# Giving every step of a decoder layer its own moment in the order of each engine's queue, and loading the ffn weights earlier

## The reference

```python
x = x + attn(layernorm(x))           # 16 heads of 8; k and v from a latent of 32; rope; causal softmax
x = x + xattn(layernorm(x), ctx)     # 8 heads of 64 over 32 context rows
x = x + ffn(layernorm(x))            # fp4 quantise-dequantise of x, weights and hidden; silu(gate) * up; 352 wide
# fp4: scale = max(max|block of 16| / 6, 1e-12); q = nearest of the fp4 grid to x / scale, times scale
```

## Time and profile before

| | us |
|---|---|
| timed runs, median (lowest to highest) | 427.41 (425.4 to 429.64) |
| profiled execution, first to last instruction | 431.1 |
| first maxima of slot 0 on TensorE | 34.59 |
| first scores of slot 0 on TensorE | 47.19 |
| last store's data ready | 429 |

### The profile page before, as it was taken

How to read it: one execution, slowest core, us unless ns; L and a number is a source line. 1 busy time by engine, 2 the same in 40 slices (tenths; PEclk the granted TensorE clock), 3 DMA queues, 4 the chain that set the end, 5 groups by cost and what they waited for, 6 DMA issues and landing times.

```text
span 431.1 us, 6518 instructions
## 1 busy us (share of the span) xinstructions
PE 295.3 (69%) x1790; PEld 144.0 (33%) x1790; DVE 301.2 (70%) x1137; ACT 177.1 (41%) x327; POOL 194.2 (45%) x374
## 2 busy tenths in 40 slices
PE   1702655777888788787868687787878846657454
PEld 1300233332343222324333334344343314436233
DVE  5426749472666546878886898989978356787872
ACT  5320345563544454443555454454446313222111
POOL 4200216761133534545384745535447353745653
PEclk9999999996766655886997798989969869766696
DMA  6079000043030025002100260030000000000000
GB/s 186 0 207 209 1 0 2 2 149 74 1 75 1 0 76 147 2 2 59 23 8 0 81 149 6 3 79 3 9 6 2 8 0 8 6 1 7 2 13 18
DMA packets 20835, 17.50 MB, mean 41 GB/s; under 512 B 1920, under 2 KB 20224, under 8 KB 20800
## 3 DMA queue, kind: packets, MB, share of 16 engines
q1 hardware_dynamic: 20272, 16.50, 15.7%
q10 hardware_dynamic: 528, 0.59, 0.5%
HBM read 9.62 MB, written 7.34 MB: 39 GB/s over the span
## 4 chain that ended last, share of the span: by engine, by line
PE 36%; DVE 30%; issue 10%; POOL 9%; DMA 7%; ACT 5%; SPq 1%; POOLq 0%; DVEq 0%; ACTq 0%
DVE summed L832 7%; PE pvp L1116 7%; PE st L1105 4%; PE mxp L1081 4%; DMA ks<-parts_dram 3%; PE mxp L1016 3%; DVE space L766 2%; PE misc L1180 2%; DMA parts_dram<-parts 2%; POOL space L473 2%; DVE space L763 2%; PE misc L1195 2%; PE pvp L1127 2%; DVE space L746 2%; ACT probs L633 2%
## 5 line engine op out<-in xcount | busy, mean ns | idle before, releaser
L832 DVE CUSTOM_DVE_ANT_0 summed<-mxp,causal 128x512 bf16<-128x512 f32 (+3 forms) x256 | 114.0, 485 | 28.2 <-PE mxp L1081 27.9
L633 ACT ACTIVATE probs<-st 128x1024 f32<-128x1024 f32 (+1 forms) x96 | 84.6, 881 | 85.4 <-PE st L1105 85.1
L1081 PE MATMUL mxp<-ks,qs 48*128 48x512 bf16 (+3 forms) x256 | 41.4, 362 | 62.2 <-DVE rmax L832 38.6
L443 POOL TENSOR_SCALAR_AFFINE_SELECT probs<-probs 128x256 f32<-128x256 f32 x128 | 49.6, 423 | 24.8 <-ACT probs L633 24.8
L1116 PE MATMUL pvp<-probs,va 128*32 128x128 f32 (+3 forms) x512 | 57.1, 530 | 5.1 <-POOL probs L443 5.1
L543 ACT ACTIVATE space<-misc 128x128 f32<-128x128 f32 (+3 forms) x78 | 24.2, 327 | 50.9 <-PE misc L1136 18.0
L1105 PE MATMUL st<-qs,ks 50*128 50x512 bf16 (+3 forms) x256 | 41.7, 366 | 4.6 <-ACT probs L633 2.5
L1081 PEld LDWEIGHTS mxp<-ks,qs 48*128 48x128 bf16 x256 | 11.9, 98 | 82.6 <-DVE rmax L832 44.6
L473 POOL TENSOR_TENSOR space<-space 128x128 f32<-128x128 f32 (+2 forms) x33 | 24.8, 751 | 19.7 <-DVE space L769 19.7
L434 POOL TENSOR_SCALAR var<-mv 128x1 f32<-128x1 f32 (+1 forms) x36 | 9.1, 253 | 46.1 <-DVE mv L739 44.6
L485 POOL TENSOR_TENSOR space<-space,reciph 128x352 f32<-128x352 f32 x16 | 12.6, 786 | 35.1 <-DVE reciph L757 35.1
(11 more groups left out here) (196 smaller groups left out, 587.9 us busy)
## 6 DMA issues: line engine op xcount, KB each, us to landing
parts_dram<-parts SPq DMA_DIRECT2D x8, 384.0 KB, 2.6
qs<-parts_dram SPq DMA_DIRECT2D x16, 192.0 KB, 3.8
ks<-parts_dram SPq DMA_DIRECT2D x16, 192.0 KB, 4.4
parts_dram<-parts SPq DMA_DIRECT2D x8, 256.0 KB, 2.9
xin<-in_x SPq DMA_DIRECT2D x4, 256.0 KB, 6.2
parts_dram<-parts SPq DMA_DIRECT2D x8, 128.0 KB, 2.9
out<-outr SPq DMA_DIRECT2D x16, 64.0 KB, 1.6
qs<-nrows SPq DMA_DIRECT2D x32, 4.0 KB
```

The costliest lines, as they stand in the source:

```text
L443: last = g.affine_select(out=m, in_=m, compare_op=ALU.is_ge, fill=0.0, base=0, pattern=[[0, 2], [1, P]], channel_multiplier=-1)
L633: nc.scalar.activation(probs[n % 2][:, 2 * pair:2 * pair + 2, 512 * k:512 * k + w], st2[:, :].rearrange("p (h q) -> p h q", h=2)[:, :, 0:w ...
L832: last = v.tensor_tensor_reduce(out=summed[:, m % 2, e * w:(e + 1) * w], in0=mxp[m % 3][:, e * w:(e + 1) * w], in1=causal[:, S - w:S], sca ...
L1081: last = mm(units[r][:, e * w:(e + 1) * w], qs[rows, c, i * P:(i + 1) * P], ks[rows, c, 0:w], start=True, stop=True)
```

## The change

1. The ten steps of a slot become 100 ticks (`T`), and every piece has a tick of its own in a table. `START` is tick -500, `END` 2200. Each engine walks the ticks and issues what is due; pieces of one tick go in a written order. A tick is no time: it only says what comes ahead of what on an engine.
2. The groups are taken apart, so that other work can stand between their steps: `row_stats` into statistics and moments, `block_scale` into `block_max`, `block_scale`, `block_recip`, `round_fp4` into `exponent`, `rounding`, `add_rounding`, `finish_fp4` into `round_off` and `scale_back`, `rstd_of` into `variance` and `deviation`, `max_parts` into two, `normalise` into two. No instruction is added or dropped.
3. The last four row blocks have a table of their own (`ROW_AT_END`), and slots 14 and 15 have one for their values.
4. The projection of batch 0, the maxima of slot 0, the ffn weights' fp4 and the set-up steps stand in the tables too: set-up steps 0 to 5 come ahead of slot 0's maxima, 6 and 7 among them, 8 and 9 around the first scores, 10 in slot 1.
5. SyncE issues the ffn weights and the x of batches 1 to 3 ahead of the store of batch 0's parts.

```diff
-STAGGER = 2
-LEAD = 6
+T = 100
...
+PAIR_AT = [-120, -105, -85, -75, -62, -52]
+MAX_AT = [-108, -107, -104, -99, -88, -79, -73, -69, -64, -58, -51, -47]
+PARTS_AT = [-31, -27]
+TURN_AT, NROWS_AT, PLACE_AT = -26, -26, -67
+SCORE_AT = [16, 34, 48, 68, 79, 104]
+EXP_AT = [21, 40, 54, 68, 83, 108]
+MASK_AT = [15, 87]
...
+PROJECT_AT_0 = {"stats": -88, "mv": -36, "var": 51, "rstd": 64, "xn": 1, "xnT_mm": -51, "xnT": -96, "lat_mm": -39,
+                "lat": -66, "rope0": 55, "cos0": 132, "swap0": -49, "sin0": 141, "lat_stats": 76, "lat_mv": 123,
+                "lat_var": 182, "lat_rstd": 234, "latn": 133, "latT_mm": 55, "latT": 6, "rope1": 115, "cos1": 182,
+                "swap1": 138, "sin1": 192, "sum0": 151, "high0": 28, "rest0": 167, "mid0": 58, "low0": 185, "sum1": 193,
+                "high1": 191, "rest1": 193, "mid1": 198, "low1": 195, "store0": 219, "store1": 290, "stacks0": 290,
+                "stacks1": 314, "values": 125, "va": 158}
...
+ROW_AT = {"attT_mm": 27, "attT": 25, "o_mm": 44, "x1": 43, "stats2": 54, "mv2": 67, "var2": 21, "rstd2": 35, "x1b": 10,
+          "xn2": 83, "xn2T_mm": 82, "xn2T": 80, "sim": 106, "xmax": 105, "xsh": 110, "xexp": 125, "xden": 132, "xrden":
+          135, "xprob": 93, "xprobT_mm": 157, "xprobT": 161, "xo": 166, "x2": 178, "stats3": 182, "mv3": 187, "var3":
+          152, "rstd3": 152, "xn3": 193, "maxx": 195, "scalex": 198, "recipx": 200, "normx": 171, "expx": 209, "clampx":
+          212, "sumx": 215, "roundx": 184, "dqx": 184, "dqxT_mm": 234, "dqxT": 237, "gate": 247, "tanh": 249, "gated":
+          251, "up": 264, "hid": 266, "maxh": 270, "scaleh": 272, "reciph": 276, "normh": 247, "exph": 289, "clamph":
+          290, "sumh": 292, "roundh": 264, "dqh": 266, "dqhT_mm": 313, "dqhT": 314, "down": 321, "outr": 326, "out": 360}
...
+ROW_FIRST = [497, 598, 698, 798, 897, 998, 1098, 1198, 1297, 1396, 1496, 1598, 1640, 1660, 1675, 1696]
+
+SET_UP_AT = [-221, -188, -182, -166, -154, -138, -99, -50, -19, 3, 139]
+WEIGHT_AT = {"va0": -335, "va1": -217, "sorted": -355, "clear": -263, "max": -235, "scale": -230, "recip": -176, "norm":
+             -108, "exp": -143, "clamp": -139, "sum": -114, "round": -93, "dq": -88}
+START, END = -T * (NG + 1), T * (NSLOT + 6)
...
+        due_rows = by_tick((ROW_FIRST[k] + at, (k, step)) for k in range(B * NT)
+                           for step, at in (ROW_AT if k < LAST else ROW_AT_END).items())
+        due_batches = by_tick((T * NG * (b - 1) + at, (b, step)) for b in range(B)
+                              for step, at in (PROJECT_AT if b else PROJECT_AT_0).items())
...
-            store_parts(0, 0)
-            store_parts(0, 1)
-            for half in range(2):
-                load_stacks(0, half)
             for at, src in ((0, L0_ffn_w_gate), (3 * P, L0_ffn_w_up)):
...
-            for n in range(NSLOT + 5):
-                b, g = n // NG, n % NG
-                for u in range(10):
-                    if u == MAX_PARTS and in_range(n + 1):
-                        max_parts(n + 1)
...
+            for tick in range(START, END):
+                for n, i in due_slots["parts"].get(tick, ()):
+                    (max_high, max_low)[i](n)
...
+                for k, step in due_rows.get(tick, ()):
+                    row(k, step)
+                for b, step in due_batches.get(tick, ()):
+                    project(b, step)
+                for step in due_weights.get(tick, ()):
+                    weights(step)
+                for n, m in due_slots["max"].get(tick, ()):
+                    max_unit(n, m)
```

More of the change, by code:

```diff
@@ L395, in _ @@
                 load_x(b)
[L396 to L408 removed]
+            for tick in range(START, END):
+                for n, _ in due_slots["place"].get(tick, ()):
+                    place_max(n)
+                for b, step in due_batches.get(tick, ()):
+                    for side in range(2):
+                        if step == f"store{side}":
+                            store_parts(b, side)
+                    for half in range(2):
+                        if step == f"stacks{half}":
+                            load_stacks(b, half)
+                for k, step in due_rows.get(tick, ()):
+                    if step == "out":
+                        store(k)
             for t in range(NT):
@@ L929, in stage_d @@
+                if step == "outr":
                     dve.wait_ge(s["down_mm"], k + 1)
@@ L1017, in project @@
                             .then_inc(s["rope_mm"], 1)
+                if step == "values":
+                    values_in(b)
             def values_in(b):
@@ L1189, in stage_d @@
                     last.then_inc(s["dqhT_mm"], 1)
-                if u == 2:
+                if step == "down":
                     pe.wait_ge(s["dqhT_d"], k + 1)
```

572 lines of the change are left out of this document (275 added, 297 removed), and 7 rows, old and new, of tables (PROJECT_AT, WHEN).

## The result

| | median of the timed runs (lowest to highest), us | against the kernel before, 95% interval |
|---|---|---|
| before, same chip | 428.52 (425.4 to 432.92) | |
| after | 357.28 (355.35 to 359.71) | 0.8356 (0.8289 to 0.8424) |

The change takes 71 us off. Three of the kernels built later have no interval, since their four executions lay in groups 2 to 3% apart; of these only the lowest and the highest time are read.

The account below looks back on a forecast made before the run. No engine bounds the whole span; VectorE does in slots 7 to 14, elsewhere mostly queues waiting for each other. Terms +2.0, -8, -1, -9.5, -5.7 sum to -22.2, taking 427.4 to 405 us; range 387 to 423.

Parts of the forecast that it names:

- Start, +2.0: Up to the first maxima: set-up steps 0 to 5 queued ahead delay the first pair; +2.0 us, bounds 0 and +3.
- no engine has one of its own chain steps moved behind another: At the start: the chain ending in batch 0's stacks keeps its steps and order on each engine; no cost expected.
- Slots 0 to 3, -8: Set-up steps leave these slots, freeing TensorE and VectorE; two thirds of the bound -12.6 us, the other bound -1.
- the set-up was hidden already: Rival for slots 0 to 3: TensorE idles there anyway, so -8 becomes -1; 412 us, chance 0.13.
- Slots 7 to 14, -9.5: VectorE, 87% busy, gains by parting dependent steps; two thirds of 14.4 us, the lower bound 0.
- The gap of 0.12 us and the count: VectorE, slots 7 to 14: parting saves up to 0.12 us at each of 120 neighbours, 14.4 us at most.
- the gaps don't close: Rival on VectorE: parting saves nothing or becomes other waits; terms 9.5 and 3.5 go, 418 us, chance 0.13.
- Nothing in the new order of TensorE, GpSimd or SyncE has a wait ahead of something that is due earlier: Slots 7 to 14: reordered pieces on these engines have their inputs in time; no cost was put on them.
- a -1 for slots 4 to 6: No set-up there and VectorE not the bound; fourteen dependent pairs parted, -1 us, bounds +3 and -4.
- a third of the neighbours for the tail: After the last slot: 88 of 122 dependent VectorE neighbours parted, a third of up to 10.6 us taken, -3.5.
- Tail, -5.7: After 327.4 us: GpSimd's shorter period (-2.2) and parted VectorE neighbours (-3.5); together -5.7 us, bounds 0 and -12.
- The GpSimd step: Last four row blocks: the next block's `normh` ahead of `roundh` removes GpSimd's idle; -2.2 us, bounds 0 and -4.2.

Follow-up runs that it names:

- old_newsetup: The new program with tables giving the old order, but set-up and ffn weights' steps at their new early ticks: 426.5 us, ratio 0.983 to the kernel before.
- held: The changed kernel, order untouched, with each formerly grouped VectorE step also waiting on the VectorE step directly in front: 378.1 us, ratio 0.872 to the kernel before.
- old_parted: The new program with tables giving the old order, plus only the parting of dependent VectorE neighbours: 439.3 us (431.2 to 440.1).
- normh_late: The changed kernel with GpSimd's `normh` of the last four row blocks back behind the last step of the block before: 357.2 us, ratio 0.832.
- glued: The changed kernel with the eight groups of VectorE row steps put together again, each at its first step's tick: 376.3 us (369.3 to 377.6).
- slots_old: The changed kernel with all slot pieces (maxima, scores, masks, values) at old ticks, except the last two slots' values: 437.3 us, ratio 1.023 to the kernel before.
- idle_waits: The changed kernel with additional VectorE waits, each on the VectorE step two in front, which is over by then: 360.3 us, ratio 0.834.
- setup_later: The changed kernel with set-up steps 4 to 9 moved behind the first pair of maxima: 350.8 us, ratio 0.818 to the kernel before.
- slots_old_p13: The changed kernel with slot pieces in their old pattern, all 13 ticks later together: 428.0 us, ratio 0.985 to the kernel before.
- setup_old: The changed kernel with set-up and the ffn weights' fp4 back at their old steps, weight loads still early: 366.4 us, ratio 0.847.

## Why the prediction was right in sign and wrong in size

**Start, +2.0.** It measured +4.8. The set-up chain was added up rightly (14.7 for 14.4 us), the wait that hid it too. What I missed is 1.35 us by which the projection's own chain came later, and some 1.3 between the first pair and the first scores, where steps 6 and 7 stand with 1.93 us each and 8 and 9 with 0.85, for which I had allowed 0.5 together. The 1.35 us failed at "no engine has one of its own chain steps moved behind another": that is true, but GpSimd's two memsets were moved beside one.

**Slots 0 to 3, -8.** The mechanism is right: old_newsetup gives 12.6 there, the whole of the bound of which I took two thirds. In the new order it gives 18.0, more than TensorE's time for the steps; that each set-up step holds up more in tighter queues is a guess. The rival "the set-up was hidden already" is dead.

**Slots 7 to 14, -9.5.** The gap of 0.12 us and the count come out right: the timelines give 14.6 for my 14.4. That held gives 14.6 back too is partly luck, since 4.2 of it are idle. Taking two thirds for waits that would appear was wrong for this order and right for another: on the old order (old_parted) the waits take it all, and the rival "the gaps don't close" would have been the answer. I had no step in the argument that told the two apart.

**The step that failed** is the one in which I counted the places at nothing: "Nothing in the new order of TensorE, GpSimd or SyncE has a wait ahead of something that is due earlier", followed by a term for VectorE's neighbours alone, a -1 for slots 4 to 6, and a third of the neighbours for the tail. I checked that the new order adds no wait, and never asked which of the old waits it takes away. VectorE's idle between 117.3 and the end was 66 us before (20.6, 15.7 and 30.0 in the three stages) and is 32 after (11.3, 4.3 and 16.0): 35 us, more than all the terms of my sum together. I had the windows that show the room and read them as a bound on what the neighbours could give, not as the thing at stake. VectorE's list of waits over these three stages (engine, what, for whom: us in total, times, longest) names what went. Before, then after:

```profile
DVE xmax L879 <- PE misc L1152: 10.8, 8, 3.7
DVE turned L777 <- PE mxp L1016: 8.6, 4, 3.4
DVE space L918 <- PE misc L1180: 6.5, 6, 2.8
DVE summed L832 <- PE mxp L1081: 5.7, 6, 2.7
```

```profile
DVE summed L870 <- PE mxp L1126: 10.5, 15, 2.8
...
DVE space L974 <- PE misc L1219: 2.5, 4, 1.0
...
DVE turned L788 <- PE mxp L1059: 2.3, 3, 1.1
```

The wait of the cross attention's maximum (`xmax`) is gone, those of the rope (`turned`) and of `hid` (L918, then L974) fell by 6.3 and 4.0 us, and that of the maxima units (`summed`) rose by 4.8. None of these had a term in these stages.

TensorE's clock is not shown to have a share. In the profiled executions the granted clock of slots 4 to 6 and 7 to 14 rose from 0.63 and 0.87 to 0.71 and 0.92. But the four executions of the kernel after had mean granted clocks of 0.826 to 0.904, and the fastest of them, 355.4 us, had 0.826.

**Tail, -5.7.** It measured -22.4. The GpSimd step works as described and is worth nothing measurable (normh_late). I had let it run beside VectorE's rounding at no cost, and the rounding went from 0.34 us to 0.55, 0.82 and twice 1.05. Parting gives 7 to 10 (glued, held), near my upper bound. The rest is places: slots_old still has a tail of 86.4 with the slots' tables old, so some 17 of the 22.4 us are in the tables of the rows and of the last slots' values, the parting among them.

**Adding up.** My sum treats the parts as independent. The runs say so only of the set-up: 6 to 9 us alone, 5 to 9 with the rest. Parting is worth 12 to 20 with the new places and nothing without; the slot's three kinds of pieces, put back one at a time, cost some 120 to 130 us and together 80.

## What to carry to other kernels

For a change that re-places most pieces of in-order queues, list the old kernel's cross-engine waits stage by stage and ask of each whether its producer's lead over its consumer grew: the room is that idle time, not the sum of the edits. Parting dependent neighbours on VectorE is worth up to 0.12 us each, but done alone on the old order it turned into waits. Ask also what each moved piece now runs beside: two GpSimd memsets beside four VectorE steps cost 1.3 us of the start. And don't price such tables one row at a time: a piece put back alone can cost more than all of them put back.

## What the runs showed of the hardware

A semaphore wait that is already satisfied costs VectorE nothing measurable (idle_waits, a ratio of 0.834 for 0.836). One on the step directly in front costs about 0.1 us by keeping the two apart (held, 11.3 us at 116 places).

TensorE's busy time for the same 1790 instructions lay between 264.7 us (setup_later) and 310.4 (slots_old_p13), 295.3 in the kernel before. The granted clock doesn't account for it: at mean clocks of 0.819 (setup_old) and 0.836 (before) TensorE was busy 266.2 and 295.3 us. What else does isn't shown.

VectorE and GpSimd hold each other up. VectorE's rounding of 128x352 (L763 before, L769 after) takes 0.30 to 0.35 us in 14 of 16 cases before and 11 of 16 after, and in none of these had GpSimd begun a step on a tile of 128 columns or more just ahead of it. In the other seven it had, 0.07 to 0.29 us ahead, and in all seven the rounding ended 0.20 us after GpSimd's step did. In the last blocks of the kernel after this makes 0.55, 0.82 and twice 1.05 us. Here is one of the kernel before, then the shortest and the first of the longest in the last blocks after, the latter beside the GpSimd row at 344.43 above:

```profile
414.37 0.34 DVE L763 TENSOR_SCALAR space<-space 128x352 int32<-128x352 int32 x1 [0.75 <-POOL space L485]
```

```profile
338.36 0.55 DVE L769 TENSOR_SCALAR space<-space 128x352 int32<-128x352 int32 x1
...
344.50 1.05 DVE L769 TENSOR_SCALAR space<-space 128x352 int32<-128x352 int32 x1 [0.25 <-POOL space L508]
```

GpSimd's own multiplication (L508) takes 0.94 us for 0.79 in these blocks. The first `xn` steps beside the two memsets at the start are held up too, though there the first ends 0.08 us after the memsets. Taking GpSimd's step away takes the delay away: in normh_late the four last roundings take 0.34 to 0.35 us, and in the kernel before each `xn` step 0.34. It may be a part of why GpSimd's shorter period gave nothing.

The Trainium skill, page "SBUF — State Buffer", section "Who interferes with whom", has an exclusive lock between VectorE and GpSimd; these rows agree with it.
